# Who normalises the rows: VectorE or GpSimd, in a transformer block on one core

## The reference, cut to what matters

```python
def _layernorm(x, axis=-1, eps=1e-05):
    m = jnp.mean(x, axis=axis, keepdims=True)
    v = jnp.var(x, axis=axis, keepdims=True)
    return (x - m) / jnp.sqrt(v + eps)

x = L0_attn_x                                   # (8, 256, 256)
x = x + _L0_attn_ref(_layernorm(x), wq, wk, wv, wo)      # 16 heads of 128, rotary, causal
x = x + _L0_ffn_ref(_layernorm(x), gate_w, w1, w3, w2, sw1, sw3, sw2)   # router, 2 of 8 experts, shared
```

## Time and profile before

| | us |
|---|---|
| median of 3 runs | 745.26 |
| lowest and highest | 744.40 and 746.28 |
| the profiled execution | 743.42 |
| its span in the trace | 741.6 |
| VectorE busy | 629.1 |
| GpSimd busy | 513.0 |

### The profile page before, as it was taken

The page is one execution under the profiler, slowest core; times in us unless marked ns, Lnnn a source line. Parts: engine busy times, 40 slices in busy tenths (PEclk is TensorE's granted clock), DMA queues, the critical chain, the costliest instruction groups (busy, mean ns, idle before and its releaser), DMA issues.

```text
span 741.6 us, 16481 instructions
## 1 busy us (share of the span) xinstructions
PE 716.5 (97%) x5481; PEld 686.0 (93%) x5481; DVE 629.1 (85%) x1787; ACT 535.0 (72%) x1683; POOL 513.0 (69%) x536
## 2 busy tenths in 40 slices
PE   4899999999999999999999999999999989999998
PEld 4787999999999999999999999999999979999997
DVE  5898889998998889889989988989898956866567
ACT  5788777777777777777777777777677755666564
POOL 5878667777777777877787778777866724544554
PEclk9999999999999999999999999999999999999999
DMA  6554202331323133213321321130454364344392
GB/s 209 141 170 142 95 25 94 124 132 35 107 107 117 44 111 111 104 45 126 110 93 41 137 104 60 37 106 30 142 194 176 138 214 134 120 130 132 104 310 82
DMA packets 49484, 85.92 MB, mean 116 GB/s; under 512 B 8440, under 2 KB 40152, under 8 KB 47800
## 3 DMA queue, kind: packets, MB, share of 16 engines
q1 hardware_dynamic: 45352, 73.44, 29.8%
q0 software_dynamic: 4048, 11.42, 4.3%
HBM read 60.12 MB, written 44.59 MB: 141 GB/s over the span
## 4 chain that ended last, share of the span: by engine, by line
PE 83%; DVE 8%; ACT 4%; POOL 2%; issue 2%; DMA 1%; SPq 0%; ACTq 0%; POOLq 0%; DVEq 0%
PE bank L652 64%; PE bank L692 5%; PE bank L685 3%; PE bank L701 3%; DVE work L1027 2%; PE bank L890 1%; PE bank L871 1%; DVE work L1020 1%; ACT work L1437 1%; PE bank L800 1%; POOL work L480 1%; DVE w_lo L994 1%; PE bank L846 1%; ACT w_hi L1420 1%; PE bank L907 1%
## 5 line engine op out<-in xcount | busy, mean ns | idle before, releaser
L1642 POOL TENSOR_TENSOR qkt_lo<-work,qkt_hi 128x512 fp32r<-128x512 f32 x128 | 166.0, 1297 | 84.3 <-ACT qkt_hi L1430 84.3
L480 POOL TENSOR_TENSOR work<-work 128x512 f32<-128x512 f32 x127 | 165.2, 1301 | 47.3 <-DVE work L1027 44.2
L1027 DVE TENSOR_TENSOR work<-bank,sinn 64x512 f32<-64x512 f32 x256 | 176.1, 688 | 3.4
L1430 ACT CAST qkt_hi<-work 128x512 fp32r<-128x512 f32 x128 | 79.6, 622 | 96.3 <-POOL work L480 94.4
L652 PE MATMUL bank<-xnt_hi,w_lo 128*128 128x256 f32 x512 | 146.3, 286 | 2.1 <-DVE xnt_lo L1058 2.1
L652 PE MATMUL bank<-xnt_lo,w_hi 128*128 128x256 f32 x512 | 145.8, 285 | 0.0
L652 PE MATMUL bank<-xnt_hi,w_hi 128*128 128x256 f32 x512 | 145.8, 285 | 0.0
L1437 ACT ACTIVATE work<-work,bias 128x128 f32<-128x128 f32 (+1 forms) x256 | 112.7, 441 | 0.0
L1020 DVE TENSOR_TENSOR work<-bank,cosn 128x512 f32<-128x512 f32 x128 | 88.1, 688 | 18.9 <-PE bank L652 18.5
L652 PEld LDWEIGHTS bank<-xnt_hi,w_lo 128*128 128x128 f32 x512 | 98.8, 193 | 2.9 <-DVE xnt_lo L1058 2.9
L652 PEld LDWEIGHTS bank<-xnt_hi,w_hi 128*128 128x128 f32 x512 | 99.1, 194 | 0.0
(11 more groups left out here) (191 smaller groups left out, 2124.3 us busy)
## 6 DMA issues: line engine op xcount, KB each, us to landing
rows_by_expert<-in_zero_t SPq DMA_DIRECT2D x17, 1028.0 KB
weights_split<-stage SPq DMA_DIRECT2D x40, 176.0 KB, 1.9
w_lo<-weights_split SPq DMA_DIRECT2D x4, 1408.0 KB, 10.3
w_lo<-results_by_token SPq DMA_DIRECT2D x16, 256.0 KB, 5.1
w_lo<-rows_by_expert SPq DMA_DIRECT2D x24, 128.5 KB, 2.2
w_hi<-weights_split SPq DMA_DIRECT2D x2, 1536.0 KB, 6.7
stage<-in_L_ffn_w SPq DMA_DIRECT2D x32, 88.0 KB, 2.2
weights_split<-stage SPq DMA_DIRECT2D x20, 128.0 KB, 1.9
```

Source lines behind the costliest of these rows:

```text
L480: eng.tensor_tensor(roped[:, a], rope_cos[:, a], rope_sin[:, a], ALU.add).then_inc(rope_add, 1)
L1027: op = nc.vector.tensor_tensor(rope_sin[lo:lo + 64, a], p_qk[a][hi:hi + 64, :, :], sn, ALU.mult)
L1430: nc.scalar.copy(qkt[a][0][:, :, :], roped[:, a]).then_inc(qkt_hi, 1)
L1642: nc.gpsimd.tensor_tensor(qkt[a][1][:, :, :], roped[:, a], qkt[a][0][:, :, :], ALU.subtract).then_inc(qkt_lo, 1)
```

## The change

GpSimd gets a function `centre`, which does one pair, and calls it at two places: at head 2 right behind its `rsqrt`, for the router's rows (sequences 1 to 7), and at head 9 between `choose` and `low`, for the next sequence's rows (sequences 1 to 6). VectorE does these pairs no longer; it keeps the ones of sequence 0 and that of the last sequence's router rows, in the tail. Since `mv` is now read by GpSimd, VectorE waits for the readers before it writes it again, at heads 1 and 5, and GpSimd waits at head 9 for VectorE's last reading of the scratch in `xn`.

```diff
@@ VectorE, sequence(b)
                     if b is not FIRST:
                         if h == 1:
                             rows_stats(b, b - 1)
+                            dve.wait_ge(xn_done, b + 1)
                             rows_mv(b)
-                        if h == 2:
-                            rows_norm(b, b - 1)
...
                         if h == 5:
+                            if b is not FIRST:
+                                dve.wait_ge(xn2_done, b)
                             norm_mv(b + 1)
-                        if h == 9:
+                        if h == 9 and b is FIRST:
                             norm_x(b + 1)
@@ GpSimd
+            def centre(rows, b, done):
+                for t in range(ST):
+                    op = nc.gpsimd.tensor_scalar(rows[:, t], resid[:, b * ST + t, :], mv[:, t, 0:1], rstd[:, t:t + 1],
+                                                 ALU.subtract, ALU.mult)
+                op.then_inc(done, 1)
+
...
                         if h == 9:
                             choose(b)
+                            if b is not LAST:
+                                pool.wait_ge(rank_done, b)
+                                pool.wait_ge(rstd_done, b + 2)
+                                centre(xn[:, :, :], b + 1, xn_done)
...
                         if h == 2:
                             rsqrt(mv2_done, vare2_done, rstd2_done, b, ST)
+                            pool.wait_ge(rstd2_done, b)
+                            centre(xn2[:, :, 0:D], b - 1, xn2_done)
```

## The result

| | before | after |
|---|---|---|
| median (us), of 4 runs each on one chip | 745.39 | 768.19 |
| lowest and highest | 744.40 and 746.28 | 766.62 and 768.93 |
| the profiled execution | 743.42 | 768.93 |
| its span | 741.6 | 767.1 |

The ratio is 1.0304 (95%: 1.0288 to 1.0320): the changed kernel is 22.8 us slower.

What follows compares the result with a forecast made beforehand. TensorE was taken as the bound, sometimes waiting for VectorE. Holds at heads 10 and 4 less a 2.3 us gain gave 13 C - 11.5 = +1.5 us, so 746.8 us, called the same; range 743.2 to 752.8.

Steps and rivals of the forecast that it cites:

- C: Time of one moved pair on GpSimd, first instruction's start to second's end; taken as 1.0 us, range 0.65 to 1.46.
- the formula: Whole kernel: 6 (C - 0.77) + 7 (C - 0.65) - 2.3 = 13 C - 11.5 us, +1.5 for C = 1.0.
- The slack at the two places: Heads 9 and 2: TensorE is held only for C beyond 0.77 us (six times) and 0.65 us (seven times).
- Who is waited for: Heads 10 and 4: the scores' weight load waits for GpSimd's `qkt_lo`, 0.2 to 0.4 us, 13 times.
- Its path ends no later than GpSimd's: Behind the head 2 pair: ScalarE's normalising also awaits the addition, but already waits 0.26 us for VectorE's reciprocal.
- The gain: VectorE's relief: 7 x 0.2 (head 3) + 6 x 0.05 (head 10) + 0.4 + 3 x 0.08 = 2.3 us.
- the 0.4 us that the prediction took from the router's product: Router's product: half of TensorE's 0.8 us of waits there, put down to VectorE, would go.
- No DMA is moved: Transfers: none moved; the sends of heads 12 to 15 follow GpSimd's order and come, if anything, sooner.
- the prediction's own sign: Profile after: mechanism wrong if TensorE waits at heads other than 4 and 10, or GpSimd's 1.30 us operations lengthen.
- The second: Rival: TensorE waits for GpSimd at heads 10 and 4; C = 1.46 gives +7.5 us, 752.8; slower, chance 0.42.
- The first: Rival: pairs nearly all hidden on GpSimd, C at most 0.65; only the gain stays, -2.3 us, 743.0; chance 0.11.
- the third: Rival: losses at heads 3 and 10 not the pairs' doing, smaller gain; 747.6, no difference; within the 0.47 chance.

Runs made afterwards that it cites:

- e5: Kernel before plus 21 lone GpSimd instructions of seven forms at its end, executed once for durations; the moved form takes 1.23 us with VectorE idle.
- e3: The change with GpSimd doing only the first tile of each pair, VectorE the second; 752.68 us against 744.57 for the kernel before, 1.0098.
- e9: Kernel before with the 13 pairs on ScalarE, their shift on GpSimd, and SyncE's next piece load ahead of the stores; 741.49 us against 744.82, 0.9963.
- e8: Kernel before with SyncE loading the next piece of expert weights ahead of the stores of the piece just split; 744.10 us against 744.82, 0.9989.
- the swap: SyncE's next piece load put ahead of the stores, in three kernels; ratio 0.9989 on the kernel before, 1.0263 on the change (1.0304 without).
- e7: Kernel before with the 13 pairs on ScalarE, their shift made by two short GpSimd instructions; 745.26 us against 744.37, 1.0006.

## Why the prediction was wrong

**The size of C: wrong, and it is enough for the whole miss.** The step that failed was to bound C from above by the two-input operation of the same width, 0.73 to 0.83 us an instruction, as if one input could not cost more than two, and then to take half of that operation's growth per column, C = 1.0. The instruction takes 1.22 us, 1.5 to 1.7 times these rows, and e5 shows the two beside each other, 725 and 1234 ns. What was taken for the cheaper form is the dearer one: the rows before held no GpSimd instruction of the kind `tensor_scalar` wider than 128x2, and none of its relatives could bound it. The bounds were two rows of other kinds, not bounds of this one. 13 x (2.45 - 1.0) = 18.9 us of the 21.3 between the forecast +1.5 and +22.8 come from this term; the formula with the measured C gives 765.7, far outside the range.

The Trainium skill ("GPSIMD Engine Reference", § 4.1 Engine selection) has one-input work on GpSimd roughly at line rate, from which the prediction estimated C = 0.8, or 0.40 an instruction. The copy agrees, with 0.40 us for 256 columns and 0.84 ns for each further one; `tensor_scalar` with 0.86 to 1.23 us doesn't. The Trainium skill (the same page, § 8 Key points) has VectorE about twice as fast at elementwise work; the +9.3 us that the prediction worked out from it came nearer than its own sum, and was too mild as well: 1.22 against 0.40 us is three times.

**The slack at the two places: right, within 0.15 us a time.** 0.77 and 0.65 us were read from before. The half pair (e3), which goes just beyond them, changed head 10 by 0.39 us a time where 0.40 followed; with the whole pair head 10 has 1.48 where 1.63 followed, and heads 3 and 4 1.58 where 1.60 did.

**Who is waited for: right in the end, not in the row.** The holds come at these two places, seven and six times. But at the first TensorE stops one step sooner, for ScalarE's normalising. "Its path ends no later than GpSimd's" is true of its end (the scores' load starts 0.06 us after the subtraction's end), yet 1.40 of the hold's 1.74 us are spent in waiting for ScalarE.

**The gain: right in its sum, in part by luck.** Waits for `pt_lo` fell from 4.0 to 1.4 us. e9, which keeps the gain without the cost, has -1.4 us at head 3 (7 x 0.2, as forecast), -0.6 at head 10 (forecast -0.3) and -0.3 at head 1 (forecast -0.24), and it is 2.6 us faster than e8, for a forecast of 2.3. But the 0.4 us that the prediction took from the router's product were not VectorE's to give: in e8, where VectorE keeps all its pairs, the waits there are gone (its view of weight-load waits has the row of `pt_lo` alone, 4.0 us as before), and e9 has no more at head 5 than e8 (-0.4 both). They were the load's. VectorE's busy time fell by 11.8 us where 16 were forecast. The pairs' own two lines fell by 15.7 us; part of that time overlapped other instructions (in the earlier trace rows `pt_lo` starts before the pair ends), and busy time counts an overlap once.

**"No DMA is moved": wrong.** None is moved in the program, but loads and stores of the pieces hang on the split that stands behind the pair on GpSimd. By the prediction's own sign TensorE was not to wait at heads other than 4 and 10, and it does at 5, 11 and 12. This route costs 3.6 us in the change by the steps; by the ratios the swap is worth 3.1 us there (0.0041 of 745) and 0.8 in the kernel before.

**The rivals.** The second, in which TensorE waits for GpSimd, is what happened, but at 1.22 us an instruction in place of its 0.73, so that its own +7.5 us was a third of the loss. The first and the third are out.

**What stays open.** Why TensorE's clock falls at head 14 of sequence 7 in some executions and not in others, and why `tensor_scalar` costs GpSimd so much is not known from these runs. The steps are from one execution of each kernel.

## What to carry to other kernels

A bound for an operation that the trace lacks holds only if the row is of the same form on the same engine; otherwise measure the form by itself first, or leave the upper end open. The slack of an engine, even one that is only 70% busy, is read at the place, from the idle time before its late instruction to the moment at which it is needed, and here TensorE paid in full for what went beyond it. Look for the engine that waits at that very place (ScalarE here), follow its queue to every tile that stands behind the wait, and ask which transfers hang on what stands behind the new work.

## What the runs showed of the hardware

- On GpSimd, 128x256 fp32: copy 0.40 us, `tensor_tensor` 0.72, the same with a spread column 0.61, `tensor_scalar` 0.86 (one constant) to 1.23 us (two steps, two columns), and 2.08 for 512 columns. A subtraction of a column is thus cheaper as a `tensor_tensor` with the column spread (0.61) than as a `tensor_scalar` (1.01). VectorE does the full two-step form in 0.40.
- A VectorE instruction on 128x2 with both inputs in SBUF took 0.42 us at best and 1.03 beside a GpSimd addition, ending with it. The Trainium skill ("SBUF — State Buffer", § Who interferes with whom) says that a VectorE instruction with two SBUF inputs contends with a GpSimd instruction that reads SBUF, for ports that they share under an exclusive lock. The trace agrees: VectorE's was over only when the addition was, small as it is. GpSimd made the same numbers in two instructions of 0.19 to 0.20 us (e7).
- GpSimd's own 1.30 us operations did not become longer when its work moved: L480 is 1.30 us in the mean, before and after.
- With TensorE's granted clock at its lower level for 3.4 us, head 14 of sequence 7 took 1.55 to 1.58 us longer, in four profiles.
- Five stores issued by SyncE take 2.2 to 2.3 us of its queue. Putting a load ahead of them was worth 0.1% alone and 0.4% where another engine had used up the slack.
